# Double queries two slots later, one statistics fill earlier, and the stacking transfers one slot later

## What is computed

```python
x = x + _L0_xattn_ref(_layernorm(x, axis=-1), ctx_1024, mask_Bx1xSxS2_fk0, ...)
x = x + _L0_ffn_ref(_layernorm(x, axis=-1), L0_ffn_w_freq_real, L0_ffn_w_freq_imag, L0_ffn_bias)

# _L0_xattn_ref, with q, k, v = projections split into 16 heads
score = jnp.einsum('bhqd,bhkd->bhqk', q, k) / jnp.sqrt(KEY_SIZE)
score = score * mask
score = jnp.where(score == 0, -1000000000.0, score)
alignment = jax.nn.softmax(score, axis=-1)
context = jnp.einsum('bhqk,bhkd->bhqd', alignment, v)
return context @ wo_w + wo_b

# _L0_ffn_ref
x_freq = jnp.fft.fft(x, axis=-1)
y_freq = jnp.einsum('bnd,do->bno', x_freq, w)
return jnp.real(jnp.fft.ifft(y_freq, axis=-1)) + bias
```

## Time and profile before

| | us |
|---|---|
| median of 3 runs | 457.08 (456.91 to 457.08) |
| the profiled execution | 456.98 |
| its span, first to last instruction | 455.2 |

### The profile page before, as it was taken

How to read it: one execution, slowest core, us unless ns; L and a number is a source line. 1 busy time by engine, 2 the same in 40 slices (tenths; PEclk the granted TensorE clock), 3 DMA queues, 4 the chain that set the end, 5 groups by cost and what they waited for, 6 DMA issues and landing times.

```text
span 455.2 us, 10923 instructions
## 1 busy us (share of the span) xinstructions
PE 433.3 (95%) x3510; PEld 298.5 (66%) x3510; DVE 403.5 (89%) x538; ACT 368.3 (81%) x1342; POOL 353.0 (78%) x476
## 2 busy tenths in 40 slices
PE   6989897998999999999999999999999999989997
PEld 5777676777566676666676666666766665555444
DVE  3797699889999999999999999999999899999353
ACT  3358597789998989998989899899989899999620
POOL 6588844685879989798989898989899877755763
PEclk9999999999999999999999999999999999999999
DMA  8996662332426455564555445546443424341244
GB/s 287 389 376 183 234 199 70 93 92 60 107 72 153 109 156 115 141 133 125 117 153 117 132 87 138 128 123 153 108 104 66 109 69 115 55 92 24 71 110 122
DMA packets 85287, 60.15 MB, mean 132 GB/s; under 512 B 40142, under 2 KB 72814, under 8 KB 84719
## 3 DMA queue, kind: packets, MB, share of 16 engines
q1 hardware_dynamic: 84508, 59.29, 48.4%
q10 hardware_dynamic: 722, 0.17, 0.2%
HBM read 29.33 MB, written 8.39 MB: 83 GB/s over the span
## 4 chain that ended last, share of the span: by engine, by line
PE 58%; DVE 14%; POOL 10%; issue 8%; ACT 7%; DMA 1%; ACTq 1%; POOLq 0%; DVEq 0%
PE bank L454 24%; PE bank L459 15%; PE bank L611 7%; ACT zs L714 5%; PE bank L625 4%; DVE zs L904 4%; PE scores L599 3%; DVE zs L897 3%; PE bank L560 2%; POOL cl L1146 2%; POOL rzb L1140 2%; POOL xs L1093 2%; ACT pt L723 1%; PE bank L541 1%; DMA bqb<-in_bq 1%
## 5 line engine op out<-in xcount | busy, mean ns | idle before, releaser
L714 ACT ACTIVATE zs<-zs,nbias 128x128 f32<-128x128 f32 x512 | 199.5, 395 | 18.1 <-POOL nbias L1133 17.3
L714 ACT ACTIVATION_READ_ACCUMULATOR zs<-zs,nbias 128x1 f32 x512 | 98.4, 192 | 0.0
L904 DVE SCALAR_TENSOR_TENSOR zs<-zs 128x1024 f32<-128x1024 f32 x64 | 89.7, 1401 | 1.2
L909 DVE TENSOR_REDUCE nmin<-zs 128x8 f32<-128x1024 f32 x64 | 78.1, 1220 | 2.2
L897 DVE TENSOR_TENSOR zs<-scores,ms 128x1024 f32<-128x1024 f32 x64 | 78.1, 1220 | 1.0 <-issue 0.6
L723 ACT COPY pt<-bank 128x512 f32<-128x512 f32 x128 | 67.8, 580 | 13.5 <-PE bank L611 13.4
L611 PE MATMUL bank<-ident,zs 128*128 128x128 f32 x512 | 66.8, 273 | 1.9 <-ACT zs L714 1.9
L459 PE MATMUL bank<-xth,wqh 128*128 128x256 f16 x224 | 61.2, 273 | 1.3 <-DVE ql L869 1.3
L1093 POOL TENSOR_TENSOR xs<-xs,bob 128x512 f32<-128x512 f32 (+1 forms) x41 | 42.9, 1049 | 25.0 <-DVE zs L904 21.9
L459 PE MATMUL bank<-xtl,wqh 128*128 128x256 f16 x224 | 61.1, 273 | 0.0
L459 PE MATMUL bank<-xth,wql 128*128 128x256 f16 x224 | 61.1, 273 | 0.0
(11 more groups left out here) (126 smaller groups left out, 929.2 us busy)
## 6 DMA issues: line engine op xcount, KB each, us to landing
xs<-in_x SPq DMA_DIRECT2D x16, 512.0 KB, 4.5
xtr<-in_xt SPq DMA_DIRECT2D x16, 512.0 KB, 4.5
out<-x SPq DMA_DIRECT2D x31, 256.0 KB, 2.5
qs<-qh SPq DMA_DIRECT2D x120, 64.0 KB
lp<-in_lparts SPq DMA_DIRECT2D x4, 1024.0 KB, 8.3
qs<-ql SPq DMA_DIRECT2D x60, 64.0 KB
ms<-in_mask SPq DMA_DIRECT2D x16, 128.0 KB, 2.6
wqs<-in_wq SPq DMA_DIRECT2D x2, 512.0 KB, 6.9
```

The lines of the kernel that those rows point to most:

```text
L714: last = act.activation(z, z, ACT.Exp, bias=nbias[:, s % 4, i:i + 1], scale=-NEG, accum_out=zsum[:, s % 4, i:i + 1])
L904: dve.scalar_tensor_tensor(out=z, in0=z, scalar=0.0, in1=z, op0=ALU.is_equal, op1=ALU.subtract).then_inc(eq_done, 1)
L909: dve.tensor_reduce(nmin[:, s % 4, :], zs[:, s % NZ].rearrange("p t h k -> p (t h) k"), AX.X, ALU.min).then_inc(mn_done, 1)
```

## The change

The double queries of chunks 3 to 15 move. That of chunk 3 is in slots 5 and 7 (it was 5 and 6), that of chunk c from 4 on in slots 4c - 7 and 4c - 5. So slot 6 has none any more and slot 55 has one. The fill ST of chunk 4 moves from slot 10 to slot 7. On SP the stack of chunk c from 3 on is issued in the queue's part for slot 4c - 4, behind the transposes, the mask, the store and the load of xt, in place of the end of the part for slot 4c - 5.

```diff
-    queries = {2: (2, 0), 4: (2, 1), 5: (3, 0), 6: (3, 1)}
+    queries = {2: (2, 0), 4: (2, 1)}
@@
         if v in queries:
             late.append(("QQ",) + queries[v])
-        elif v >= 7 and v % 2 == 1 and (v + 9) // 4 < NC:
-            late.append(("QQ", (v + 9) // 4, (v + 9) % 4 // 2))
+        elif v >= 5 and v % 2 == 1 and (v + 7) // 4 < NC:
+            late.append(("QQ", (v + 7) // 4, (v + 7) % 4 // 2))
@@
 def row_slot(c):
-    return {3: 3, 4: 10}.get(c, 4 * c - 9)
+    return 4 * c - 9
@@
                 if r == 0 and 5 <= c + 4 < NC:
                     load_xt(c + 4)
+                if r == 0 and 3 <= c + 1 < NC:
+                    stack_q(c + 1)
                 if r == 3 and 0 <= c - 2 < NC - 1:
                     turn_x1n(c - 2, 0)
@@
                 if r == 3 and 0 <= c - 3 < NC:
                     store(c - 3, 0)
-                if r == 3 and 3 <= c + 2 < NC:
-                    stack_q(c + 2)
```

## The result

| | before | after |
|---|---|---|
| median, us | 457.04 (456.91 to 457.08) | 460.47 (460.21 to 461.84) |
| profiled execution | 456.98 | 460.29 |
| its span | 455.2 | 458.5 |

The ratio is 1.0082 (95% interval 1.0061 to 1.0102): 3.4 us slower, where 456.4 was forecast with a range up to 458.0. The busy shares tell little, as before (page, part 1, to be held against the earlier trace rows): TensorE is 3.2 us busier with the same 3510 instructions, so the same list of work took it longer.

A forecast was written before the change was run, and what follows sets the result against it. VectorE was taken to hold the pace up to slot 13 and from slot 54, TensorE between. 456.98 - 2.7 (front) + 2.0 (tail) = 456.3, or 456.4 us on the median's scale, range 455.0 to 458.0.

The forecast's parts named there:

- the front: Slots up to 13, where VectorE holds the pace: slot 6 loses a double query, 2.7 us gained at slot 14.
- the tail: From slot 54 on: slot 55 gains a double query, VectorE waits for it in slot 56, 2.0 us lost.
- allowance in slots 10 to 12: Front: 0.4 us more gain, since TensorE's 1.71 us wait before the ST of chunk 4 is gone.
- The scores of slot 7 need the score banks: TensorE, slot 7: scores start once banks are free at 80.14, so slot 8 starts at 84.5, a gain of 2.5 us.
- M of slot 8: TensorE's product M comes 2.5 us earlier, so VectorE's 0.76 us wait for its copy shrinks; VectorE leaves about 2.4 early.
- Rival C: GpSimd, busy from 98.60 to 108.37, caps the front's gain at 1.5 us, giving 457.6 us; chance 0.15.
- The walk: Slot-by-slot dating of the front's instructions after the change, ending 2.7 us early at slot 14.
- the surest part: VectorE, slot 7: a 1.33 us wait and 0.61 us low half go; slot 8's mask product gains 1.9 us.
- Moving ST costs 0.13 us: Chunk 4's fill adds 0.13 us in slot 7 and removes as much in slot 10; its inputs are ready.
- The steady part and the transfers: Two TensorE-bound slots stay at 12.05 us; later stacks land with 2.2 to 4.1 us of cover, costing nothing.
- Rival B: Stack lands too late for the scores of slot 4c-1, 11 times the lateness, 461.9 to 481 us; chance 0.09.
- The shift by the load of xt: SP: an xt load directly ahead of the stack could delay it 4.5 us; held that only the first transfers shift.

The follow-up runs named there:

- halves, copy and constant row early, short additions: Changed kernel, chunk 2's stack issued in two halves, GpSimd's rzb copy and constant row moved earlier, slot 7's two additions cut to 8 columns: 456.69 us.
- halves, copy and constant row early: Changed kernel, chunk 2's stack issued in two halves, GpSimd's rzb copy and constant row moved ahead of its additions in slot 7: 457.46 us.
- halves: Changed kernel, chunk 2's stack issued in two halves, each with its own semaphore: 458.19 us.
- changed, U twice: Changed kernel, TensorE computes the product U of slot 7 twice, filling 1.7 us of idle time: 458.9 us.
- the version that kept the query in that place: Changed kernel, chunk 3's second query kept in slot 6, none in slot 7, last double query split, chunk 15's stack in halves: 456.38 us.
- the version with the short last query: Changed kernel, last double query in slot 55 runs 6 of its 24 matmuls: 459.31 us.

## Why the prediction was wrong

The forecast was 2.7 us gained in the front and 2.0 lost in the tail. The front came out 1.4 late, the tail as told. The gain at slot 14, in a line of versions, each with one hindrance less than the one below it:

| version | slot 14 early by, us | what the step is |
|---|---|---|
| forecast | 2.7 | |
| halves, copy and constant row early, short additions | 2.28 | allowance in slots 10 to 12: 0.4 |
| halves, copy and constant row early | 1.56 | GpSimd beside VectorE in slot 8: 0.7 |
| halves | 0.82 | M waits for GpSimd's row: 0.7 |
| changed, U twice | 0.14 | the wait for chunk 2's stack: 0.7 |
| changed | -1.42 | the clock's fall after it: 1.6 |

Together 4.1 us, which is what lies between 456.4 and 460.5. The copy's place alone moved nothing (0.8), so the 0.7 of the row's step is the row's. The shares belong to this order of removing: with chunk 2's wait gone slot 8 is 2.35 early in place of 0.20, and how much of these 2.15 us arrives at slot 14 depends on what else is in the way.

- "The scores of slot 7 need the score banks, which VectorE's mask product of slot 7 (78.92, 1.22 us) leaves at 80.14": this step failed. It is right as far as it goes (80.47 in the version with halves), but the scores of step 4c also need the stack, and step 8 is such a step. The text before the prediction says that the scores in slot 4c - 1 wait for all 14 transfers, and slot 7 is 4c - 1 for c = 2; the transfers were weighed for chunks 14 and 15 and not for the one whose slot came 4 us earlier. The scores started at 82.50, not 80.14. In the table the price of this without the clock is only 0.7 us, since most of what TensorE loses there it would have lost again in slots 8 to 11, to GpSimd.
- No step dealt with the clock: the granted clock was 1.00 in every stretch read, and an idle time of 2.9 us ahead of dense work was not foreseen. That is the largest term, 1.6 us, and it hangs on the step above.
- M of slot 8, "which TensorE computes without a gap after its slot start", and therefore 2.5 early: M also needs a row that GpSimd writes in its slot 8. Rival C named GpSimd as what caps the front and put it at 98.60 to 108.37 through ScalarE's biases; it caps it at 88.8, through a row of constants (0.7 us), and by slowing VectorE (0.7 us). The walk moved instructions and kept their durations: L904 took 2.32 us in place of 1.47 once it fell beside GpSimd's additions.
- VectorE's own part, "the surest part": right for its first instruction only. The mask product of slot 8 starts at 84.56, 2.01 early, where 1.33 + 0.61 = 1.94 was forecast. What it gained ended in a wait of 2.76 us for ScalarE's high half three instructions later.
- "I allow 0.4" for slots 10 to 12: with all the hindrances removed slots 8 to 13 are 2.35 early alike (slot 11 more, on TensorE alone). The wait before the ST of chunk 4 did go, but nothing of it was passed on.
- "Moving ST costs 0.13 us": no run contradicts it in the changed kernel, but alone the move delays slot 8 by 0.87 us, of which 0.28 is the fill's duration and 0.58 the bank's turn.
- The tail: right in place, cause and size. L869 waits 1.35 us (1.4), the next instruction and all behind it come 2.05 later (2.0), and none is given back: at TensorE's slot 64 it is 2.02.
- The steady part and the transfers: right. Two slots take 12.10, four 24.10, and no scores behind slot 7 wait for a stack. Rival B, the slow one, did happen in its kind, scores that wait for a stack, but in the one chunk for which the change doesn't move it.
- The shift by the load of xt did not come. The Trainium skill's rule of ring order ("DMA: Bandwidth & Descriptors", section "Queues, rings and completion order") is not refuted by that: in the steady stretch the scores started without a wait behind such a load, which shows only that whatever the load delays is over before the scores need the last of the 14 transfers.

## What to carry to other kernels

Before work is moved to an earlier time, list every semaphore that it waits for, those too that never cost anything, and date each from its own row: a dependence that is half a microsecond from binding has no line in any view of waits. Where a walk makes two engines' instructions meet that were apart, their durations are not constants, and the neighbour's list deserves a walk of its own. A gap ahead of dense work has a second price in the clock: here the clock took over twice as much as the wait, and the version that kept the query in that place had the lowest time of all.

## What the runs showed of the hardware

- After 2.92 us of idle time TensorE's clock went from full to half 0.7 us into the work that followed (by the stretches, 0.39 / 0.5 = 0.8 us of low clock before 84.00), for 3.4 us; in one execution with a gap of 2.96 us it fell during the gap, for 6.8 us. After 1.22 us of idle time it stayed full in the profiled execution. The fall costs 1.6 us in the traces and about 2 us in the times of the version with the short last query, and the spread of that version's times goes with it.
- Such a fall is not the gap's alone. Of 35 executions of the kernel before that were measured beside the first four versions, three have a mean clock of 0.996 and took 458.9 to 459.5 us, against a median of 457.2; the version with the halves, whose wait at that place is 0.64 us, has one of twelve (460.8). No trace shows where the clock fell in these. What the gap does is to make the fall the rule: all four executions of the changed kernel have a mean clock of 0.996 or less, the slowest (461.84 us) 0.993.
- VectorE's L904, which reads the same 128x1024 fp32 tile as both its inputs, takes 1.22 us with GpSimd idle (at 80.67 in the kernel before), 1.47 beside the end of GpSimd's copy, and 2.32 and 3.12 us beside GpSimd's additions; GpSimd's copy of 128x512 takes 0.61 or 1.61, its two additions 2.49 or 3.49. The Trainium skill ("GPSIMD Engine Reference", section "1. Specifications") says that GpSimd's interfaces to the on-chip memory are shared with VectorE and that VectorE's instructions with two inputs from there contend. The trace agrees, and adds the price: up to 1.9 us on a 1.2 us instruction.
- The rows look like turns, not like sharing. L904 ends 1.07 to 1.09 us after the GpSimd instruction that it met has ended, whatever its own length: the copy ends at 88.23 and L904 at 89.30 in the kernel before, the additions at 87.06 and L904 at 88.14 in the changed kernel, 87.31 and 88.39 with the halves, 87.91 and 89.00 with the constant row early. In turn GpSimd's next instruction there (L1088), 0.22 us with the halves, takes 1.19 and ends at 89.08, right behind L904. No run tests this reading by itself, and GpSimd's spans are rough.
